# A mixture-of-experts layer: the gate travels with the token's row, and the experts' results are added up in DRAM by the scatters

## The chip, the cores and the metric

The kernel runs on one core of a Trainium2 chip. Its engines are TensorE (PE in the profile, PEld its weight loads), VectorE (DVE), ScalarE (ACT), GpSimd (POOL) and SyncE (SP), which here issues transfers and nothing else. The metric is the device time of one execution in microseconds (us); lower is better.

## What is computed

One transformer layer on `x` of 4 x 1024 tokens with 128 values each, all in float32. First attention with a window of 64 keys is added to `x`. Then a feed-forward part, of which this case changes the end. With `xf` the normalised tokens (N = 4096):

```python
shared = silu(xf @ sg) * (xf @ su) @ sd                  # 128 -> 256 -> 128, every token
top_scores, top_idx = top_k(masked, 4)                   # 4 of 32 experts per token
gates = softmax(top_scores)
pos = cumsum(onehot, 0)[arange(N * K), flat_e] - 1       # place in the expert's queue
keep = pos < capacity                                    # capacity = 640
buf = zeros((E + 1, capacity, d)).at[e_s, p_s].set(xf[tok])[:E]
h = silu(einsum('ecd,edh->ech', buf, wg)) * einsum('ecd,edh->ech', buf, wu)
out_e = einsum('ech,ehd->ecd', h, wd)
contrib = out_e[flat_e, minimum(pos, capacity - 1)] * (flat_g * keep)[:, None]
routed = zeros_like(xf).at[tok].add(contrib)
return x + shared + routed
```

So each of the 32 experts works on up to 640 rows, and a token's output is the sum of at most four experts' rows, each times its gate.

## The kernel before, in words

Each engine has its own program, written by hand in order, and semaphores are the only ties between them. `wait_ge(s, n)` holds an engine's queue until the semaphore has reached n. There are three stages.

**Attention and dispatch.** `attention_steps` walks over 32 tiles of 128 tokens in a software pipeline. For each tile VectorE also picks the four experts and computes the slot numbers `sidx`, and the gates into an SBUF table `gates` (L1155). The normalised row, followed by one more number that tells where its result is to go (the "pair", 4 x token + k, L435), is written by GpSimd with four indirect transfers per tile (`expert_slots<-xfe`, L447) into a table in DRAM with 640 slots of 129 values for each expert. A slot beyond the capacity is out of bounds and is dropped. Beforehand SP fills the table (L320, 32 transfers) and zeroes a second one, `pair_results` with 16384 rows of 128 (L323, 32 transfers).

**Experts.** `lagged_steps` walks over the 32 experts, with three of them in work: for the next one (`en`) TensorE transposes its rows (L875) and VectorE and ScalarE split rows and weights into high and low parts; for the present one (`e`) TensorE does gate and up (L864) in two halves, with SiLU on ScalarE (L607) and the product on VectorE (L1259); for the one before (`ed`) TensorE does the down projection (L890) into PSUM banks 6 and 7 and signals `down_done`. Then ScalarE copies the result out in two pieces (L623 of 512 columns and L625 of 128, both counting `y_evac`), between its two pairs of SiLUs. ScalarE waits there for `down_done`, and for `y_sent`, which tells that the results of two experts ago have left the same buffer. GpSimd waits for both copies and for `yidx`, the destinations as whole numbers (L1265), and issues five indirect transfers of 128 rows (L463), one for each fifth of the 640 slots. Unused slots have a destination out of bounds and are skipped. SP reloads slots, gate/up weights and down weights (L315, L308, L309, L312) in two buffers; ahead of L312 it waits for `down_done` alone.

**Last stage.** The shared expert is computed in eight steps of 512 tokens (`shared_step`). Two are done before the experts, six behind them. SP waits for all scatters and then loads `pair_results` back, four rows for each token, 16 transfers of 512 KB through four buffers (L364). VectorE's `combine` multiplies the first two rows of a token by their gates and adds them to `x_all` (L1246, four for each pair of tiles); GpSimd does the same for the other two (L474, L479, L483), and VectorE adds its sum (L1251). ScalarE's queue stores each pair of tiles (L636, 16 transfers).

## Time and profile before

| | before |
|---|---|
| three runs, us | 888.08, 897.61, 899.48 |
| median | 897.61 |
| span of the profiled execution | 904.6 |
| busy in it: TensorE, VectorE, ScalarE, GpSimd | 724.0, 534.0, 360.9, 415.1 |
| moved between DRAM and the core | 68.37 MB in 52338 packets |
| written to and read from DRAM | 39.99 and 34.89 MB |

The profiled execution is one more run of the same program. Its own time is the span, from the first to the last instruction, and what lies around it, which isn't listed; the runs are below the span by 5 to 17 us. A view that lists groups gives the busy time and the mean of one instruction, and behind the second bar the idle time of the engine just before them and what ended it. "remote" there is a release that the view can't put down to an instruction of this core. The end of a TensorE record is a model, since matmuls overlap.

### The profile page before, as it was taken

Reading aid. Unit: us, or ns where it says so; the run is one execution under the profiler, and the core shown is the slowest. Engines: PE = TensorE matmul, PEld = TensorE weight load, DVE = VectorE, ACT = ScalarE, POOL = GpSimd, SP = SyncE. Lnnn points to the kernel's source line nnn. Section 1 sums busy time; section 2 is a strip of 40 time slices with the busy share of each in tenths; the row PEclk is TensorE's granted clock in tenths of the full one; section 3 lists DMA queues with packets and bytes.
Section 4 is the critical chain, followed back from the end, with each engine's and each line's share of the span. In section 5 each row is a group of like instructions: output and inputs, shape, how many; then the busy total and the mean of one; then the engine's idle time right before and its main releaser. Section 6 shows DMA issues by size and latency. Waiting matters only on the chain.

```text
span 904.6 us, 24570 instructions
## 1 busy us (share of the span) xinstructions
PE 724.0 (80%) x7521; PEld 563.5 (62%) x7521; DVE 534.0 (59%) x2192; ACT 360.9 (40%) x853; POOL 415.1 (46%) x548
## 2 busy tenths in 40 slices
PE   3798888988978788898888858888888888877960
PEld 1565656665646565575665637777777777777540
DVE  3476756556577676656666656545454454543598
ACT  4465544454455445444454423332323232322200
POOL 4125343353343434334344350555555555556555
PEclk9698776676798878767788859999999999998985
DMA  8991000000000000000000002423233333421355
GB/s 268 358 390 35 14 20 15 12 23 12 12 22 10 20 9 15 10 7 14 6 7 6 6 8 84 125 76 105 76 114 107 114 115 103 126 75 32 122 182 167
DMA packets 52338, 68.37 MB, mean 76 GB/s; under 512 B 9505, under 2 KB 31807, under 8 KB 52304
## 3 DMA queue, kind: packets, MB, share of 16 engines
q1 hardware_dynamic: 38240, 53.56, 18.4%
q0 software_dynamic: 9216, 11.97, 4.4%
q10 hardware_dynamic: 4848, 2.40, 0.9%
q8 instruction: 19, 0.31, 0.1%
q14 instruction: 15, 0.12, 0.0%
HBM read 34.89 MB, written 39.99 MB: 83 GB/s over the span
## 4 chain that ended last, share of the span: by engine, by line
PE 52%; another core or an unknown queue 19%; issue 10%; DVE 10%; ACT 6%; POOL 1%; ACTq 1%; DVEq 1%; POOLq 0%
PE bank L693 9%; PE bank L864 7%; PE bank L680 6%; PE bank L674 5%; PE bank L663 5%; PE bank L657 3%; PE bank L701 3%; DVE x_all L1246 3%; DVE mx L1044 2%; PE bank L733 2%; ACT hact L607 2%; PE bank L817 2%; PE bank L756 1%; PE bank L747 1%
## 5 line engine op out<-in xcount | busy, mean ns | idle before, releaser
L463 POOL DMA_INDIRECT pair_results<-yout,yidx x160 | 157.2, 982 | 143.4 <-ACT yout L625 104.0
L447 POOL DMA_INDIRECT expert_slots<-xfe,sidx x128 | 127.0, 992 | 141.5 <-DVE sidx L1148 108.3
L864 PE MATMUL bank<-xgT_parts,wgu_parts 128*128 128x320 f32 x768 | 147.2, 344 | 46.4 <-ACT hact L607 46.4
L864 PEld LDWEIGHTS bank<-xgT_parts,wgu_parts 128*128 128x128 f32 x768 | 125.9, 208 | 57.3 <-ACT hact L607 50.3
L519 ACT ACTIVATE pt<-bank 128x512 f32<-128x512 f32 x128 | 76.2, 596 | 182.2 <-PE bank L680 164.9
L1259 DVE TENSOR_TENSOR hact<-hact,bank 128x320 f32<-128x320 f32 x128 | 57.1, 481 | 140.2 <-ACT hact L607 133.1
L1044 DVE TENSOR_REDUCE mx<-bank 128x4 f32<-128x512 f32 x128 | 87.3, 683 | 32.5 <-PE bank L663 19.7
L421 POOL TENSOR_TENSOR pout<-pin,mhalf 128x3 f32<-128x3 f32 (+2 forms) x36 | 29.9, 830 | 127.4 <-DVE pin L970 127.4
L890 PE MATMUL bank<-wdn,hact 128*128 128x128 f32 x640 | 82.7, 288 | 2.3 <-issue 2.3
L890 PEld LDWEIGHTS bank<-wdn,hact 128*128 128x128 f32 x640 | 82.5, 207 | 2.5 <-issue 2.5
L623 ACT COPY yout<-bank 128x512 f32<-128x512 f32 x32 | 18.7, 585 | 162.2 <-remote 151.0
L657 PE MATMUL bank<-maskq_b,ident_b 128*128 128x512 bf16 x128 | 54.2, 424 | 33.3 <-DVE mx L1044 28.8
L693 PE MATMUL bank<-pt,v_mix 128*32 128x64 f32 x1024 | 78.2, 298 | 0.0
L693 PE MATMUL bank<-pt,v_cur 128*32 128x64 f32 x1024 | 77.0, 293 | 0.0
L607 ACT ACTIVATE hact<-bank 128x320 f32<-128x320 f32 x128 | 53.5, 447 | 38.9 <-PE bank L864 36.7
L680 PE MATMUL bank<-qT,kT 64*128 64x64 bf16 x1024 | 66.7, 218 | 0.1
L674 PE MATMUL bank<-comb_mv,comb_st 112*128 112x128 bf16 x512 | 66.0, 270 | 0.1
L680 PEld LDWEIGHTS bank<-qT,kT 64*128 64x128 bf16 x1024 | 48.4, 111 | 20.2 <-issue 14.4
L663 PEld LDWEIGHTS bank<-kT,qT 64*64 64x64 bf16 x1024 | 37.3, 117 | 37.5 <-issue 37.5
L663 PE MATMUL bank<-kT,qT 64*64 64x128 bf16 x1024 | 60.3, 242 | 0.0
L693 PEld LDWEIGHTS bank<-pt,v_cur 128*32 128x32 f32 x1024 | 54.7, 164 | 0.0
L693 PEld LDWEIGHTS bank<-pt,v_mix 128*32 128x32 f32 x1024 | 49.3, 143 | 3.8
(148 smaller groups left out, 1335.1 us busy)
## 6 DMA issues: line engine op xcount, KB each, us to landing
expert_slots<-fill SPq DMA_DIRECT2D x32, 322.5 KB, 6.5
xg<-expert_slots SPq DMA_DIRECT2D x32, 322.5 KB
pair_results<-rload SPq DMA_DIRECT2D x32, 256.0 KB
rload<-pair_results SPq DMA_DIRECT2D x16, 512.0 KB, 4.0
wgu<-in_L_ffn_wg_dram SPq DMA_DIRECT2D x32, 128.0 KB
wgu<-in_L_ffn_wu_dram SPq DMA_DIRECT2D x32, 128.0 KB
wdn<-in_L_ffn_wd_dram SPq DMA_DIRECT2D x32, 128.0 KB
pair_results<-yout,yidx POOLq DMA_INDIRECT x160
```

What stands on the lines that cost most here:

```text
L447: g.indirect_dma_start(out=slots_d, out_offset=bass.IndirectOffsetOnAxis(ap=sidx[:, tr.b, k:k + 1], axis=0), in_=xfe[:, tr.b, k, :], in_of ...
L463: g.indirect_dma_start(out=pairs_d, out_offset=bass.IndirectOffsetOnAxis(ap=yidx[:, c, j:j + 1], axis=0), in_=yout[:, c, j, :], in_offset= ...
L519: a.activation(pt[:, ts.b, u], bank[2 + u % 2][:, :], ACT.Exp, scale=QK_SCALE)\
L607: a.activation(hact[:, e.b, h, ch * CH:(ch + 1) * CH], bank[2 + h][:, 0:CH], ACT.Silu)\
L657: mm(bk[:, :].rearrange("p (c j) -> p c j", c=4), ident_b[:, :], maskq_b[:, :].unsqueeze(1).broadcast_to([P, 4, P]), start=True, stop=Fals ...
L663: last = mm(bk[hb * WIN:(hb + 1) * WIN, c * P:(c + 1) * P], qT[rows, tp.b, g4 + c, hb * WIN:(hb + 1) * WIN], kT[rows, tp.b, g4 + c, hb * W ...
L674: mm(bk[:, c * P:(c + 1) * P], comb_st[0:WIN + 3 * H, NS * (g4 + c) + s, :], comb_mv[0:WIN + 3 * H, ts.b, :], start=(c == 0), stop=False, ...
L680: last = mm(bk[:, at:at + WIN], kT[rows, ts.b, g4 + c, hb * WIN:hb * WIN + P], qT[rows, ts.b, g4 + c, hb * WIN:(hb + 1) * WIN], start=Fals ...
L693: last = mm(bank[7][32 * (h % 4):32 * (h % 4 + 1), to:to + WIN], vals, pt[:, ts.b, u, at:at + WIN], start=True, stop=True)
L864: last = mm(bank[2 + 2 * w + h][:, 0:CH], wgu_parts[:, e.b, wp, w, h * P:(h + 1) * P], xgT_parts[:, e.b, xp, ch * CH:(ch + 1) * CH], start ...
L890: last = mm(bank[6 + j // 4][:, j % 4 * D:(j % 4 + 1) * D], hact[:, ed.b, h, j * P:(j + 1) * P], wdn[:, ed.b, h, :], start=(h == 0), stop= ...
L1044: v.tensor_reduce(m[:, g4:g4 + 4, s], bank[u % 2][:, :].rearrange("p (c j) -> p c j", c=4), AX.X, ALU.max).then_inc(S.p1_reduced, 1)
```

## The change

The gate of a pair no longer stays in a table. VectorE writes it into the row that is dispatched (column 129 of now 130), and in the place of the pair's number stands the token's (L435's copy now takes `token`). Empty slots are filled with the number of a spare row behind the tokens and a gate of 0. The expert's ScalarE scales each row by its gate when it copies the result out, in five pieces with the gate as the per-partition scale. The five indirect transfers of an expert then add their rows to one of two tables of token sums in DRAM, the even experts to one and the odd ones to the other, and all 640 rows go each time. GpSimd waits for each piece by itself. The last stage loads two sums for each token in place of four rows, in four chunks of eight tiles, and VectorE adds them. Here is the diff, cut to its core:

```diff
-        "pair": ((np.arange(N // P)[None, :, None] * P + p[:, None, None]) * TOPK + np.arange(TOPK)).reshape(P, -1),
+        "token": p[:, None] * (N // P) + np.arange(N // P)[None, :],
+        "spare": N + np.arange(cap // P)[None, :] * P + p[:, None],
...
-    ROW = D + 1
+    ROW = D + 2
...
+    NACC, NCH = 2, 4
+    TCH = NT // NCH
+    ZEROS = NACC * (NCH + 1)
...
-    pairs_d = nc.dram_tensor("pair_results", [N * TOPK, D], F32, kind="Internal").ap()
+    sums_d = [nc.dram_tensor(f"token_sums{a}", [N + cap, D], F32, kind="Internal").ap() for a in range(NACC)]
+    sums_v = [d[0:N, :].rearrange("(p q t) d -> p q (t d)", p=P, q=NCH) for d in sums_d]
...
-            with sp.Fori(0, NT) as t:
-                sp.dma_start(pairs_v[t], rload[:, 0].rearrange("p k d -> p (k d)")).then_inc(S.zeroed, 16)
+            for a in range(NACC):
+                for q in range(NCH):
+                    sp.dma_start(sums_v[a][:, q, :], sums[:, 0, 0].rearrange("p t d -> p (t d)")).then_inc(S.zeroed, 16)
+                sp.dma_start(sums_d[a][N:N + cap, :].rearrange("(j p) d -> p j d", p=P), sums[:, 0, 0, 0:ST, :])\
+                  .then_inc(S.zeroed, 16)
...
-            for c in range(NR // 2):
-                load_results(c, c)
-            with sp.Fori(0, NT // NR - 1) as i:
-                for c in range(NR // 2):
-                    sp.wait_ge(S.comb_step, CSTEPS * ((NR // 2) * i + (c + 1)))
-                    load_results((NR // 2) * i + (NR // 2 + c), c)
+            for q in range(NCH):
+                for a in range(NACC):
+                    sp.dma_start(sums[:, q, a].rearrange("p t d -> p (t d)"), sums_v[a][:, q, :])\
+                      .then_inc(r_arrived[q], 16)
...
+                    pool.wait_ge(S.gate_done, 2 * tr.n + 2)
...
-                    pool.wait_ge(S.y_evac, 2 * e + 2)
-                    hold(pool)
                     for j in range(ST):
+                        pool.wait_ge(S.y_evac, ST * e + (j + 1))
+                        hold(pool)
                         g.indirect_dma_start(
-                            out=pairs_d, out_offset=bass.IndirectOffsetOnAxis(ap=yidx[:, c, j:j + 1], axis=0),
-                            in_=yout[:, c, j, :], in_offset=None, bounds_check=N * TOPK - 1,
-                            oob_is_err=False).then_inc(y_sent[c], 16)
+                            out=sums_d[c], out_offset=bass.IndirectOffsetOnAxis(ap=yidx[:, c, j:j + 1], axis=0),
+                            in_=yout[:, c, j, :], in_offset=None, bounds_check=N + cap - 1,
+                            oob_is_err=True, compute_op=ALU.add).then_inc(y_sent[c], 16)
...
-                    a.copy(yout[:, ed.b, 0:4], bank[6][:, :].rearrange("p (j d) -> p j d", d=D))\
-                     .then_inc(S.y_evac, 1)
-                    a.copy(yout[:, ed.b, 4:ST], bank[7][:, 0:D].rearrange("p (j d) -> p j d", d=D))\
-                     .then_inc(S.y_evac, 1)
+                    act.wait_ge(S.ypair_ready, ed.n + 1)
+                    hold(act)
+                    for j in range(ST):
+                        a.activation(yout[:, ed.b, j], bank[6 + j // 4][:, j % 4 * D:(j % 4 + 1) * D], ACT.Copy,
+                                     scale=ypair[:, ed.b, j, 1:2]).then_inc(S.y_evac, 1)
...
+            for q in range(NCH):
+                act.wait_ge(S.comb_step, 2 * q + 2)
+                act.dma_start(out_v[:, TCH * q:TCH * (q + 1), :], x_all[:, TCH * q:TCH * (q + 1), :])\
+                   .then_inc(S.stored, 16)
...
-                    v.scalar_tensor_tensor(gates[:, bass.ds(tr.n, 1), :].rearrange("p o k -> p (o k)"), ex4[:, tr.b],
-                                           exr[:, :], keep[:, :], ALU.mult, ALU.mult).then_inc(S.gate_done, 1)
+                    v.tensor_scalar(xfe[:, tr.b, :, D + 1], ex4[:, tr.b], exr[:, :], None, ALU.mult)\
+                     .then_inc(S.gate_done, 1)
...
-                    wait(dve, S.yidx_ready, en.n - 1)
-                    v.tensor_copy(ypair[:, en.b], xg[:, en.b, :, D]).then_inc(S.ypair_ready, 1)
...
+                if en is not None:
+                    wait(dve, S.yidx_ready, en.n - 1)
+                    wait(dve, S.y_evac, ST * (en.n - 1))
+                    v.tensor_copy(ypair[:, en.b], xg[:, en.b, :, D:ROW]).then_inc(S.ypair_ready, 1)
...
+            def combine(q):
+                dve.wait_ge(r_arrived[q], 16 * NACC)
+                dve.wait_ge(S.sh_added, 2 * q + 2)
+                xs = x_all[:, TCH * q:TCH * (q + 1), :]
+                for a in range(NACC):
+                    if a:
+                        dve.wait_ge(S.comb_step, NACC * q + a)
+                    v.tensor_tensor(xs, xs, sums[:, q, a], ALU.add).then_inc(S.comb_step, 1)
...
             def shared_and_combine(m, md):
                 shared_step(m, md)
-                if md is not None and md.n > SHARED_EARLY and md.n < N // 512 - 1:
-                    q = 2 * (md.n - SHARED_EARLY - 1)
-                    dve.wait_ge(S.sh_added, md.n)
-                    combine(q, q % (NR // 2), q // (NR // 2))
-                    combine(q + 1, (q + 1) % (NR // 2), (q + 1) // (NR // 2))
+                if md is not None and md.n % 2:
+                    combine(md.n // 2)
+            combine(0)
             shared_steps(shared_and_combine, SHARED_EARLY, N // 512)
```

Line numbers differ between the kernels: the copies L623 and L625 become L605, the scatter L463 becomes L460, `combine` is L1224, the shared step's product L1225 becomes L1206, its addition L1230 becomes L1211, and the SiLU L607 becomes L586.

On ScalarE this stands in the expert loop between the two pairs of SiLUs (first pair's second SiLU, copies, second pair's first). Before:

```order
L607 ACTIVATE hact<-bank 128x320 [waits gu_done]
L244 REGISTER_ALU [waits down_done]
L623 COPY yout<-bank 128x512 [waits y_sent0]
L625 COPY yout<-bank 128x128
L606 REGISTER_ALU
L607 ACTIVATE hact<-bank 128x320 [waits gu_done]
```

And now:

```order
L586 ACTIVATE hact<-bank 128x320 [waits gu_done]
L243 REGISTER_ALU [waits down_done]
L605 ACTIVATE yout<-bank,ypair 128x128 [waits y_sent0,ypair_ready]
L605 ACTIVATE yout<-bank,ypair 128x128 x4
L585 REGISTER_ALU
L586 ACTIVATE hact<-bank 128x320 [waits gu_done]
```

The two copies of different size have become five of the same, and the first of them waits for `ypair_ready` as well.

On GpSimd the expert loop reads so before, from the end of the dispatch on (the two experts of a turn):

```order
L456 UNCONDITIONAL_BRANCH [waits zeroed]
L456 ISA
L460 ISA [waits yidx_ready]
L463 DMA pair_results<-yout,yidx 16384x128 [waits y_evac]
L463 DMA pair_results<-yout,yidx 16384x128 x4
L459 REGISTER_ALU
L460 ISA [waits yidx_ready]
L463 DMA pair_results<-yout,yidx 16384x128 [waits y_evac]
```

And now, for the first of the two experts:

```order
L452 UNCONDITIONAL_BRANCH [waits zeroed]
L452 ISA
L458 ISA [waits yidx_ready]
L460 DMA token_sums<-yout,yidx 4736x128 [waits y_evac]
L458 REGISTER_ALU
L460 DMA token_sums<-yout,yidx 4736x128 [waits y_evac]
L458 REGISTER_ALU
L460 DMA token_sums<-yout,yidx 4736x128 [waits y_evac]
L458 REGISTER_ALU
L460 DMA token_sums<-yout,yidx 4736x128 [waits y_evac]
```

One wait for the copies ahead of five transfers has become a wait ahead of each, with a register step between two transfers.

On VectorE this is the way from the last expert (first row) into the last stage. Before:

```order
L1259 TENSOR_TENSOR hact<-hact,bank 128x320 [waits gu_done,h_act] x4
L1265 CAST yidx<-ypair 128x5 [waits y_sent1,ypair_ready]
L1225 TENSOR_TENSOR sact<-sact,bank 128x512 [waits sh_gu,sh_act] x4
L1230 TENSOR_TENSOR x_all<-x_all,bank 128x512 [waits sh_down]
L1225 TENSOR_TENSOR sact<-sact,bank 128x512 [waits sh_gu,sh_act] x2
L1230 TENSOR_TENSOR x_all<-x_all,bank 128x512 [waits sh_down]
L1246 SCALAR_TENSOR_TENSOR x_all<-rload,gates,x_all 128x128 [waits r_arrived0,sh_added]
L1246 SCALAR_TENSOR_TENSOR x_all<-rload,gates,x_all 128x128
L1246 SCALAR_TENSOR_TENSOR x_all<-rload,gates,x_all 128x128 [waits comb_step] x2
L1251 TENSOR_TENSOR x_all<-x_all,rload 128x256 [waits late_sum,comb_step]
```

And now:

```order
L1232 TENSOR_TENSOR hact<-hact,bank 128x320 [waits gu_done,h_act] x4
L1238 CAST yidx<-ypair 128x5 [waits y_sent1,ypair_ready]
L1224 TENSOR_TENSOR x_all<-x_all,sums 128x1024 [waits sh_added,r_arrived0]
L1224 TENSOR_TENSOR x_all<-x_all,sums 128x1024 [waits comb_step]
L1206 TENSOR_TENSOR sact<-sact,bank 128x512 [waits sh_gu,sh_act] x4
L1211 TENSOR_TENSOR x_all<-x_all,bank 128x512 [waits sh_down]
L1206 TENSOR_TENSOR sact<-sact,bank 128x512 [waits sh_gu,sh_act] x2
L1211 TENSOR_TENSOR x_all<-x_all,bank 128x512 [waits sh_down]
L1224 TENSOR_TENSOR x_all<-x_all,sums 128x1024 [waits sh_added,r_arrived1]
L1224 TENSOR_TENSOR x_all<-x_all,sums 128x1024 [waits comb_step]
```

The first two additions of loaded sums have moved ahead of all products and additions of the late shared steps; the four small multiply-adds and one addition for a pair of tiles have become two additions of 1024 columns for eight tiles.

## Rows read from the trace of the kernel before

**Rows 1.** Sums by stretch, experts and last stage: busy us of each engine, clock, DMA, GB/s

```profile
540.00:830.00 290.00, 241.05 (x1591) 224.70 (x1590) 140.10 (x355) 89.97 (x223) 151.37 (x154) 0.92 0.32 97
830.00:905.00 75.00, 40.09 (x171) 26.43 (x170) 55.01 (x101) 9.13 (x18) 41.83 (x58) 0.77 0.46 143
```

**Rows 2.** Waits, 480 to 830, and SP's: who for whom, us, times, longest

```profile
ACT yout L623 <- remote: 151.0, 29, 5.7
...
SPq L312 <- remote: 192.5, 29, 8.5
```

**Rows 3.** Timeline of one round: start, us, engine, line, names, count, idle before

```profile
653.39 0.58 ACT L623 COPY yout<-bank 128x512 f32<-128x512 f32 x1 [4.68 <-remote]
653.45 0.38 SPq L312 DMA_DIRECT2D wdn<-in_L_ffn_wd_dram  x1
653.87 0.27 ACT L625 COPY yout<-bank 128x128 f32<-128x128 f32 x1
...
654.16 0.34 SPq L315 DMA_DIRECT2D xg<-expert_slots  x1
...
654.61 0.88 DVE L1259 TENSOR_TENSOR hact<-hact,bank 128x320 f32<-128x320 f32 x2 [4.45 <-ACT hact L607]
...
654.98 0.97 POOL L463 DMA_INDIRECT pair_results<-yout,yidx  x1 [2.70 <-ACT yout L625]
...
656.57 2.39 PE L890 MATMUL bank<-wdn,hact 128*128 128x128 f32 x20
...
660.11 0.97 POOL L463 DMA_INDIRECT pair_results<-yout,yidx  x1 [0.30 <-issue]
...
660.56 0.71 PE L875 MATMUL bank<-cst,xg 128*128 128x128 f32 x5
...
662.24 0.58 ACT L623 COPY yout<-bank 128x512 f32<-128x512 f32 x1 [5.47 <-remote]
```

**Rows 4.** Timeline, the first expert behind the loop

```profile
829.03 0.97 POOL L463 DMA_INDIRECT pair_results<-yout,yidx  x1 [0.30 <-issue]
829.68 0.59 ACT L623 COPY yout<-bank 128x512 f32<-128x512 f32 x1 [2.89 <-PE bank L890]
...
831.13 0.44 ACT L607 ACTIVATE hact<-bank 128x320 f32<-128x320 f32 x1 [0.70 <-PE bank L864]
```

**Rows 5.** Timeline, last scatter, loads, and the start of two late shared steps

```profile
845.16 0.97 POOL L463 DMA_INDIRECT pair_results<-yout,yidx  x1 [0.30 <-issue]
...
845.88 1.02 PE L837 MATMUL bank<-xfT_all,sgw 128*128 128x512 f32 x2
...
847.37 45.29 SPq L364 DMA_DIRECT2D rload<-pair_results  x16
...
851.10 1.02 PE L837 MATMUL bank<-xfT_all,sgw 128*128 128x512 f32 x2
```

**Rows 6.** Groups by form: the scatters (480 to 830), VectorE in the last stage

```profile
L463 POOL DMA_INDIRECT pair_results<-yout,yidx x150 | 147.5, 983 | 137.0 <-ACT yout L625 100.0 <-issue 37.0
...
L1246 DVE SCALAR_TENSOR_TENSOR x_all<-rload,gates,x_all 128x128 f32<-128x128 f32 x32 | 18.9, 649 | 0.0
...
L1230 DVE TENSOR_TENSOR x_all<-x_all,bank 128x512 f32<-128x512 f32 x6 | 4.1, 681 | 3.1 <-PE bank L847 3.1
```

**Rows 7.** Timeline, the last instruction

```profile
901.76 0.42 DVE L1251 TENSOR_TENSOR x_all<-x_all,rload 128x256 f32 x1
```

**Rows 8.** Sums by stretch in the last stage (clock, DMA share, GB/s at the end)

```profile
850.00:856.00 6.00, 6.00 (x34) 4.09 (x33) 4.94 (x9) 1.19 (x2) 4.11 (x7) 1.00 0.76 288
...
860.00:864.00 4.00, 3.91 (x6) 1.77 (x7) 3.97 (x11) 0.60 (x1) 2.62 (x6) 0.62 0.36 131
```

**Rows 9.** DMA queues and issues: median us to landing at the end of a row

```profile
q0 software_dynamic: 9216, 11.97, 4.4%
...
rload<-pair_results SPq DMA_DIRECT2D x16, 512.0 KB, 4.0
...
wout<-in_L_attn_Wout_dram ACTq DMA_DIRECT2D x1, 64.0 KB, 3.5
```

More of the change, by code:

```diff
@@ L136, in block_kernel @@
         numbers = field("numbers")
-        pair = field("pair").rearrange("p (t k) -> p t k", k=TOPK)
+        token = field("token")
+        spare = field("spare")
         wqkv = sb("wqkv", [P, 3 * D])
```

79 lines of the change are left out of this document (16 added, 63 removed).

## The prediction, made before the changed kernel was run

> **What bounds the kernel now.** I read the spans first, then the sums by stretch, the list of waits, the timeline of the expert loop, the groups by form and the timeline of the last stage. The profiled span is 904.6 us; the three runs took 888.08 to 899.48 us with median 897.61, which is 7.0 below the span. I make my sum against the span and take 7.0 off. Attention and dispatch fill the time up to 540 us, and nothing in the change sits on their path. The experts fill 540 to 830, the last stage 830 to 905, where TensorE is busy for 40 of 75 us and VectorE for 55 [rows 1].
>
> In the expert loop one expert takes 8.9 us: from the first copy of ScalarE (L623) at 653.39 to the next at 662.24 [rows 3]. TensorE's records end long before that: the down projections run from 656.57 to 658.96, the transposes of the next expert end at 661.3, yet ScalarE sits until 662.24 [rows 3]. The list of waits gives ScalarE 29 such waits, 151.0 us, with a releaser called "remote", and the load of the down weights on SP's queue 29 as well [rows 2]. What both wait for is `down_done`, the semaphore of the last down matmul: SP's L312 starts within 0.06 us of L623 and has no other wait there [rows 3]. So it is TensorE's signal that comes late. When does it come? The five scatters (L463) start 1.59 us after L623 and then every 1.28 us. The fifth ends at 661.08, and 1.16 us later ScalarE goes on [rows 3]. At 829.68, the first expert behind the loop, the copy is released by its down matmul while a batch is still going; but the next SiLU (L607) is then held until 831.13, 1.13 us after that batch's last scatter ends at 830.00 [rows 4]. And the last scatter of all ends at 846.13 and has landed when SP issues its loads at 847.37, 1.24 us later [rows 5]. I read from this that a batch of scatters in flight holds TensorE's signals back until it has landed. The round is a ring then: copy, 1.59 us to the first scatter, four times 1.28 and 0.97 us of scatters, 1.16 us of landing, copy. That makes 8.84 of 8.85 us.
>
> The last stage begins with that landing at 847.3. It has 16 loads of 512 KB (4.0 us to landing [rows 9]) and five additions on VectorE for each, the last one starting at 901.76 [rows 7]. Its bound is VectorE: the multiply-adds alone (L1246), 64 of about 0.6 us, take over 34 us [rows 6]. From 847.3 to 904.6 are 57.3 us.
>
> **Last stage: what changes.** Eight loads of 512 KB in place of 16, and eight additions of 128x1024. One of 128x256 with nothing beside it takes 0.42 us [rows 7], one of 128x512 0.68 us [rows 6]; the slope of 1.02 ns makes 1.2 us for 1024. So VectorE has some 10 us of additions in place of over 40, and GpSimd's multiplications go. But the order of the program moves work too. `combine(0)` now stands ahead of the six late shared steps on VectorE, and they queue behind its wait for both y_sent and two loads. Before, these steps filled that wait; the third of the late ones starts at 851.10 [rows 5]. Now TensorE will do the gate and up matmuls of one late step, begin the next and stop, since the product of the first (L1206) isn't made. I count from the landing L. The first pair of loads: 4.0, and 1.8 for the second 512 KB at the 288 GB/s of the stretch 850 to 856 [rows 8, 9], with the issue 5.9. Two additions: 8.4. Products and hand-over 0.8: 9.2. A late step takes 5.2 us, the distance from 845.88 to 851.10, and one of the four pairs of its gate and up matmuls under 1 (1.02 with its overlap) [rows 5]. So the rest of the step that stopped takes 4.4, and 2 more because TensorE has stood still, as after its pause before 860, when the granted clock was 0.62 over 4 us, a mean between 2.4 and 1.2 GHz [rows 8]. Four more steps: 20.9. The last down projections, about a third of a step: 1.9, so L + 38.4. Then 0.7 and 2.4 us of additions with hand-overs: 41.6. A store of 512 KB at the load's 4.0: L + 45.7. The last stage gets 57.3 - 45.7 = **11.6 us** shorter. It isn't halved, because TensorE becomes its bound and starts late.
>
> **Expert loop: what changes in a round.** (a) GpSimd waits for one slice instead of two copies. L625 starts 0.48 us behind L623 and is itself 128 wide [rows 3]; a first slice in its place lets the first scatter go 0.48 earlier. ScalarE first has one more wait and one more instruction that holds; I allow 0.13. Gain **0.35**. (b) Between the scatters stand a wait and a no-operation. The slices come faster (0.27 us each [rows 3]) than the scatters, so the wait is met. The gap of 0.30 may grow by 0 to 0.1; I take 0.05 four times, **0.2**. (c) Five slices of 0.27 cost ScalarE some 1.0 us with their overlap, 0.4 more than the two copies, and the SiLUs behind start so much later. In this ring TensorE has that to spare before its signals are let go: nothing; if the ring were gone, 0.4 a round. (d) The copy of `ypair` moves to the end of VectorE's step, and SP's load of the next slots waits for it. The load went at 654.16; behind the two products (L1259, to 655.49) it will go some 1.6 later. Its first use are the transposes at 660.56 [rows 3], so 4.8 us are left for a transfer of about 4. Nothing, but less than 1 us of cover is left. The wait for `y_evac` at that place is met, since the products ahead need SiLUs that follow the copies. (e) The scatter becomes an addition in DRAM. The trace has none. It has two prices: time on GpSimd and time to landing. On GpSimd the plain one takes 0.98 us [rows 6]. Low end 0 more, high end twice the work, +0.98 a scatter. I take 0, as the plain row is the nearest. To landing the low end is 0. At the high end stands a whole small transfer more, since the old sum must come out of DRAM before the new one goes in: a 64 KB load has 3.5 us from issue to landing [rows 9]. I take one more trip as long as the present landing, **1.2**, because the issue's part of the 3.5 isn't paid twice. Only the fifth scatter's counts, as the others land under their successors. All 640 rows of a batch now go, where about 57% did: 11.97 MB [rows 9] are 11,640 rows moved twice (516 and 512 bytes), and there are 20,480 slots. That lies within the range of (e).
>
> Sum of a round: -0.35 + 0.2 + 1.2 = **+1.05 us**, for 31 rounds **+32.5 us**.
>
> The Trainium skill bears on (e). Its page "DMA: Bandwidth & Descriptors" (Anatomy of one DMA) says that most of a transfer's fixed time is the wait until the target memory confirms the write. The 1.24 us behind the last scatter agree in kind; by the page's fixed 2.0 us an estimate of the extra trip would be 2.0 instead of 1.2, and the total 25 us more.
>
> **The rest.** Zeroing shrinks from 8.4 MB to 4.8, and only weight loads stand behind it that are needed after 540 us. The fill waits for one small copy on GpSimd more, behind memsets, at the very start. The gate of a tile is made on VectorE just ahead of its slot numbers, for which GpSimd waits anyway. All nothing. Total: 904.6 + 32.5 - 11.6 = 925.5, less 7.0: **919 us**.
>
> **Rivals.**
> 1. *Plain price* (faster or about the same). The addition lands as quickly as a copy. A round then gains 0.15, 31 of them 4.7; with 11.6 that is 16: 881. Should the late shared steps not wait for the loads, up to 12 more, 869. For it: the scatter's time now hardly varies. Against: the old sum must be read somewhere.
> 2. *The ring opens* (faster). Additions in flight don't hold TensorE's signals. A round is then TensorE's work, 241 us by 32 or 7.5 us [rows 1], plus (c): 7.9. Saved are 1.0 x 31 and 11.6: 855. Nothing in the trace speaks for it but that it doesn't tell why the signals wait.
> 3. *A slow landing* (slower). 2 to 3.5 us more a round in place of 1.2: 944 to 990. For it: the 3.5 us of a small load.
> 4. *A slow scatter* (slower). GpSimd takes the middle of my two ends, 1.47 us a scatter: 2.4 us a round, 76 us on the forecast, 995. From +0.2 a scatter (31 us, 950) it outweighs by far what the last stage can give. For it: the five scatters are 6.1 of the ring's 8.85 us and nothing hides them. Against: the plain row. The Trainium skill's same page gives one read and one write descriptor for an operation (SWDGE vs HWDGE vs iDMA), and has the adding unit combine two streams (SDMA does more than copy): by this three descriptors in place of two. No row here shows it.
>
> **How the numbers follow.** The forecast, with a landing 0.6 to 1.8 us longer (900 to 938): 0.34. Rival 1: 0.24. Rival 2: 0.08. Rival 3: 0.14. Rival 4 of any size: 0.20. The range for eight in ten runs from 868, which takes in rival 1, to 990, which leaves out rival 2 and the upper part of rival 4. The likeliest case's own range is 900 to 938. About 2% either way (880 to 916) can't be told from no change. Faster: rival 2, most of rival 1, whose 881 is on the line, and no more: 0.26. Same: the rest of rival 1 and the lower part of the forecast: 0.26. Slower: 0.48.
>
> **What would show it.** ScalarE's wait before L605 ends 1.2 us (rival 1) or 2.4 us (forecast) after the fifth scatter. The scatter's mean is 0.98 us (forecast) or 1.2 and more (rival 4). From one expert to the next are 9.9 us (forecast), 8.7 (rival 1) or below 8 (rival 2). In the last stage TensorE stands for some 12 us behind one late step, `combine(0)` goes first on VectorE, and the end comes 46 us after the last landing. I would be wrong most simply if TensorE's late signals have another cause than the scatters, or if the price of an addition falls on the transfer queues all along and not at the end.

## The result, and the profile after

The changed kernel took 921.0 us (median of 4 runs, 918.68 to 924.18) where the kernel before took 894.68 (4 runs): a ratio of 1.032, 95% interval 1.024 to 1.040, so it is slower. The forecast said 919. That the number agrees is luck: the mechanism behind it was another one than the forecast's, and this document is mostly about that. The two traces are compared below stretch by stretch. The execution that the trace of before shows is a long one, with a span 10 us above that kernel's median, while the span of the changed kernel is 2.8 below its own. So the traces differ by 13.6 us and the medians by 26.3, and no trace shows where the other 12.7 us lie.

First the page of the changed kernel: span, busy times, DMA queues, the chain by engine, and the groups of the scatters and of ScalarE's slices.

```profile
span 918.2 us, 24411 instructions
...
PE 729.6 (79%) x7521; PEld 569.6 (62%) x7521; DVE 499.3 (54%) x2120; ACT 387.3 (42%) x949; POOL 478.2 (52%) x501
...
q0 software_dynamic: 27136, 16.54, 14.2%
...
PE 54%; issue 16%; POOL 7%; DMA 7%; DVE 7%; ACT 5%; another core or an unknown queue 2%; POOLq 1%; DVEq 1%; ACTq 0%; SPq 0%
...
L460 POOL DMA_INDIRECT token_sums<-yout,yidx x160 | 251.7, 1573 | 68.7 <-issue 41.1
...
L605 ACT ACTIVATE yout<-bank,ypair 128x128 f32<-128x128 f32 x160 | 44.7, 371 | 91.7 <-DMA token_sums<-yout,yidx 56.7
```

A scatter takes GpSimd 1573 ns, where it took 983 [rows 6]. The queue q0 has 27,136 packets in place of 9216 [rows 9]. ScalarE's slices take 371 ns each.

Now the waits and the sums by stretch: the expert loop, the first loads of the last stage, and the rest of it. The columns are those of [rows 2] and [rows 1].

```profile
DVE yidx L1238 <- DMA token_sums<-yout,yidx: 131.8, 30, 6.3
...
ACT yout L605 <- DMA token_sums<-yout,yidx: 56.7, 17, 6.9
ACT yout L605 <- PE bank L871: 32.6, 14, 2.4
POOL token_sums L460 <- issue: 41.1, 135, 0.3
```

```profile
570.00:870.00 300.00, 226.95 (x1498) 215.45 (x1496) 126.55 (x328) 112.09 (x310) 251.55 (x160) 0.89 0.61 103
871.80:879.30 7.50, 0.00 (x0) 0.00 (x0) 0.00 (x0) 0.00 (x0) 0.00 (x0) 0.50 0.80 273
879.30:918.20 38.90, 28.81 (x134) 18.66 (x134) 21.62 (x26) 5.37 (x9) 0.00 (x0) 0.89 0.33 110
```

The "remote" waits of ScalarE in front of its copies, 151.0 us [rows 2], are gone. In their place ScalarE and VectorE wait for scatters of two experts ago, and GpSimd waits for nobody: its 160 scatters take 251.55 of 300 us, and what is left is the 0.30 us between two of them. One expert is five scatters with their gaps, 5 x (1.57 + 0.30) = 9.4 us, and from 569.96 to 871.84 are 301.9 us, 32 x 9.43. So the loop is bound by the issue of scatters on GpSimd, and no longer by a ring.

The timeline shows the same at one copy, and then the end (PE is the matmul record, the bracket is the idle time before it).

```profile
589.37 2.39 PE L871 MATMUL bank<-wdn,hact 128*128 128x128 f32 x20
590.42 1.54 POOL L460 DMA_INDIRECT token_sums<-yout,yidx  x1 [0.30 <-issue]
...
591.88 1.40 ACT L605 ACTIVATE yout<-bank,ypair 128x128 f32<-128x128 f32 x5 [2.31 <-PE bank L871]
592.26 1.54 POOL L460 DMA_INDIRECT token_sums<-yout,yidx  x1 [0.30 <-issue]
...
868.58 1.54 POOL L460 DMA_INDIRECT token_sums<-yout,yidx  x1 [0.30 <-issue]
...
871.84 4.91 SPq L364 DMA_DIRECT2D sums<-token_sums  x8
879.33 2.48 DVE L1224 TENSOR_TENSOR x_all<-x_all,sums 128x1024 f32<-128x1024 f32 x2 [25.75 <-DMA sums<-token_sums]
...
882.46 2.08 PE L821 MATMUL bank<-xfT_all,suw 128*128 128x512 f32 x2 [26.01 <-DVE sact L1206]
...
888.44 1.02 PE L818 MATMUL bank<-xfT_all,sgw 128*128 128x512 f32 x2
...
893.66 1.02 PE L818 MATMUL bank<-xfT_all,sgw 128*128 128x512 f32 x2
...
912.10 2.48 DVE L1224 TENSOR_TENSOR x_all<-x_all,sums 128x1024 f32<-128x1024 f32 x2
```

The down matmuls end at 591.76 and ScalarE starts at 591.88 while scatters follow each other without a break: here TensorE's signal is not held by scatters in flight. The last scatter ends at 870.12, and SP issues its loads at 871.84, 1.7 us later, where it was 1.24 [rows 5]. From there to the end of the span are 46.4 us, where they were 57.2.

### The profile page after: what moved, and what is told of

Its sections match the earlier page's. It is cut to its first block, busy times and chain, and to the rows that moved or that the text cites. A ratio compares the mean times of both kernels' runs of the same rounds, so it can differ in the third digit from the quotient of the medians.

```text
span 918.2 us, 24411 instructions
## 1 busy us (share of the span) xinstructions
PE 729.6 (79%) x7521; PEld 569.6 (62%) x7521; DVE 499.3 (54%) x2120; ACT 387.3 (42%) x949; POOL 478.2 (52%) x501
## 3 DMA queue, kind: packets, MB, share of 16 engines
q0 software_dynamic: 27136, 16.54, 14.2%
## 4 chain that ended last, share of the span: by engine, by line
PE 54%; issue 16%; POOL 7%; DMA 7%; DVE 7%; ACT 5%; another core or an unknown queue 2%; POOLq 1%; DVEq 1%; ACTq 0%; SPq 0%
PE bank L674 10%; DMA token_sums<-yout,yidx 6%; PE bank L644 6%; PE bank L661 6%; POOL token_sums L460 6%; PE bank L655 6%; PE bank L845 5%; PE bank L638 4%; PE bank L682 3%; PE bank L714 2%; DVE mx L1025 2%; PE bank L871 2%; PE bank L828 2%; PE bank L821 2%
## 5 line engine op out<-in xcount | busy, mean ns | idle before, releaser
L460 POOL DMA_INDIRECT token_sums<-yout,yidx x160 | 251.7, 1573 | 68.7 <-issue 41.1
L845 PE MATMUL bank<-xgT_parts,wgu_parts 128*128 128x320 f32 x768 | 154.3, 350 | 56.6 <-DVE hact L1232 53.5
L845 PEld LDWEIGHTS bank<-xgT_parts,wgu_parts 128*128 128x128 f32 x768 | 130.7, 215 | 64.3 <-DVE hact L1232 60.1
L586 ACT ACTIVATE hact<-bank 128x320 f32<-128x320 f32 x128 | 56.2, 444 | 90.3 <-PE bank L845 89.7
L605 ACT ACTIVATE yout<-bank,ypair 128x128 f32<-128x128 f32 x160 | 44.7, 371 | 91.7 <-DMA token_sums<-yout,yidx 56.7
L674 PE MATMUL bank<-pt,v_mix 128*32 128x64 f32 x1024 | 80.3, 304 | 0.0
L674 PE MATMUL bank<-pt,v_cur 128*32 128x64 f32 x1024 | 79.4, 300 | 0.0
L1238 DVE CAST yidx<-ypair 128x5 uint32<-128x5 f32 x32 | 7.1, 222 | 131.8 <-DMA token_sums<-yout,yidx 131.8
L871 PE MATMUL bank<-wdn,hact 128*128 128x128 f32 x640 | 76.6, 275 | 0.7 <-issue 0.7
L871 PEld LDWEIGHTS bank<-wdn,hact 128*128 128x128 f32 x640 | 75.0, 192 | 0.9 <-issue 0.9
```

The lines of the kernel that those rows point to most:

```text
L460: g.indirect_dma_start(out=sums_d[c], out_offset=bass.IndirectOffsetOnAxis(ap=yidx[:, c, j:j + 1], axis=0), in_=yout[:, c, j, :], in_offse ...
L674: last = mm(bank[7][32 * (h % 4):32 * (h % 4 + 1), to:to + WIN], vals, pt[:, ts.b, u, at:at + WIN], start=True, stop=True)
L845: last = mm(bank[2 + 2 * w + h][:, 0:CH], wgu_parts[:, e.b, wp, w, h * P:(h + 1) * P], xgT_parts[:, e.b, xp, ch * CH:(ch + 1) * CH], start ...
L871: last = mm(bank[6 + j // 4][:, j % 4 * D:(j % 4 + 1) * D], hact[:, ed.b, h, j * P:(j + 1) * P], wdn[:, ed.b, h, :], start=(h == 0), stop= ...
```

## The experiments

**The kernels ran under other conditions than in the first comparison.** In all three later comparisons the kernel before took 725 to 726 us, not 895. So the kernel before and the changed one were run again, unchanged, and each experiment is held against these.

Two lengths will tell nearly everything: the *loop*, from the first scatter of the results to SP's first load of the last stage, and the *last stage*, from there to the end of the span. They are differences of times in each timeline.

| kernel | us, median | ratio to before (95%) | first scatter | loop | last stage |
|---|---|---|---|---|---|
| before, first comparison | 894.7 | | 566.0 | 281.4 | 57.2 |
| changed, first comparison | 921.0 | 1.032 (1.024 to 1.040) | 570.0 | 301.9 | 46.4 |
| before_again | 725.3 | | 456.7 | 209.6 | 57.2 |
| after_again | 804.8 | 1.109 (1.103 to 1.116) | 453.8 | 302.0 | 45.5 |
| after_copy | 712.4 | 0.981 (0.975 to 0.986) | 456.3 | 212.5 | 45.8 |
| after_half | 804.9 | | 457.5 | 300.0 | 45.6 |
| after_four | 743.1 | 1.022 (1.015 to 1.029) | 456.4 | 240.0 | 45.7 |
| after_late | 792.2 | 1.092 (1.086 to 1.098) | 455.0 | 303.6 | 32.3 |
| before_pieces | 722.6 | 0.996 (0.993 to 0.999) | 457.0 | 207.7 | 56.4 |
| before_four | 715.5 | 0.987 (0.982 to 0.993) | 456.4 | 199.9 | 57.2 |
| before_two | 714.1 | 0.985 (0.979 to 0.991) | 451.3 | 196.8 | 60.7 |
| gated_pairs | 705.8 | 0.975 (0.968 to 0.981) | 453.9 | 213.2 | 36.2 |
| gated_again | 704.9 | 0.968 (0.963 to 0.974) | 462.0 | 211.8 | 36.3 |

The last three columns are read from one trace of each kernel. The loop of after_again and that of after_late are the same code and differ by 1.6 us, so a difference of 2 or 3 us between two loops is hardly more than scatter.

**1. Both kernels again.** No edit.

> The kernel before, unchanged, for its trace where it takes 725 us and not 895. Theory A (the ring belongs to the first comparison alone: there a wait of TensorE's signals until the scatters had landed stood in the trace; here the kernel is 170 us faster): the waits for a releaser that the trace cannot name, 19% of the chain of before, are gone, the expert loop takes 6.5 to 6.7 us a round in place of 8.85, TensorE is its bound, and the last stage still takes 57 us. Theory B (all of it is a higher clock of TensorE from the start): the unnamed releaser keeps its share, and the round is 8 us or more.

> The changed kernel, unchanged, under the same conditions as the other experiments. Theory A (GpSimd's 5 x 1.88 = 9.4 us bounds its round in either condition; the kernel before is bound by TensorE at 6.6 us a round here): the loop takes 300 us as with the combining step placed late, the last stage 46 us, so about 804 us, 1.11 of before. Theory B (placing the combining step late has cost time, and not saved any): 780 us or less.

Both theories A held. First the kernel before in the first comparison: the chain by engine, and a stretch of attention in the sums by stretch.

```profile
PE 52%; another core or an unknown queue 19%; issue 10%; DVE 10%; ACT 6%; POOL 1%; ACTq 1%; DVEq 1%; POOLq 0%
```

```profile
100.00:400.00 300.00, 255.69 (x3323) 180.16 (x3322) 194.81 (x1011) 148.17 (x353) 125.18 (x187) 0.78 0.05 15
```

The same kernel in before_again: chain and scatters of its page, the sums of the same stretch and of the expert loop, and the timeline of one copy.

```profile
PE 47%; issue 20%; DVE 12%; POOL 10%; ACT 5%; DMA 4%; DVEq 1%; POOLq 1%; ACTq 0%; SPq 0%
...
L463 POOL DMA_INDIRECT pair_results<-yout,yidx x160 | 157.4, 984 | 72.2 <-issue 47.4
```

```profile
100.00:400.00 300.00, 273.74 (x4480) 194.19 (x4474) 273.59 (x1343) 194.01 (x470) 169.63 (x251) 0.99 0.06 17
457.00:665.00 208.00, 203.60 (x1520) 195.67 (x1518) 132.90 (x331) 93.68 (x216) 157.08 (x161) 1.00 0.43 127
```

```profile
458.94 2.39 PE L890 MATMUL bank<-wdn,hact 128*128 128x128 f32 x20
...
460.50 1.26 POOL L463 DMA_INDIRECT pair_results<-yout,yidx  x1 [0.30 <-issue]
461.37 0.59 ACT L623 COPY yout<-bank 128x512 f32<-128x512 f32 x1 [2.23 <-PE bank L890]
```

In the first comparison, two of the waits of attention with the unnamed releaser, the first from before and the second from the changed kernel:

```profile
ACT pt L519 <- remote: 17.2, 5, 4.1
```

```profile
ACT oT L526 <- remote: 7.9, 4, 2.6
```

In before_again the unnamed releaser is gone from the chain. A scatter lasts as long as before (984 against 983 ns), but the same 300 us of attention hold 4480 matmuls in place of 3323, with a granted clock of 0.99 in place of 0.78. The down matmuls end at 461.33, a scatter is being issued, and the copy starts at 461.37. So plain scatters in flight don't hold TensorE's signal here, and TensorE is busy for 203.6 of 208 us of the loop. Of the 181 us that the kernel before is faster here, 109 lie ahead of the first scatter and 72 in the loop; the last stage is the same 57.2. The changed kernel gains ahead of the first scatter only (116 us); its loop stays at 302.0 against 301.9. Up to the first scatter the kernel before had such unnamed waits in the first comparison too, on ScalarE and VectorE, 45.5 us in all, and the changed kernel 22.5; before_again and after_again have none. GpSimd's issue is a bound of its own, whatever TensorE does.

**2. The addition alone.**

```diff
                             in_=yout[:, c, j, :], in_offset=None, bounds_check=N + cap - 1,
-                            oob_is_err=True, compute_op=ALU.add).then_inc(y_sent[c], 16)
+                            oob_is_err=True).then_inc(y_sent[c], 16)
```

> The changed kernel with plain scatters: the addition is left out of them, so that of several rows for one token only the last to land stays, and the sums are not the reference's. Nothing else differs: as many scatters, rows, waits and loads. Theory A (the addition itself costs GpSimd time: 1573 ns a scatter against 983 ns before, and five scatters with their gaps, 5 x 1.88 = 9.4 us, are the round): a scatter falls back to about 0.98 us, GpSimd's part of a round to 5 x 1.28 = 6.4 us, and the round to the ring of the forecast without its landing term, 8.5 to 8.9 us, 893 to 905 us in all; if the ring stays open, the round is 7.7 us or so and the time about 869. Theory B (the scatter is longer because all 640 rows are now sent and none is skipped): it stays at 1.5 to 1.6 us and the time at 915 to 925. Theory C, my forecast's landing term (the addition costs 1.2 us where the fifth scatter lands, and nothing on GpSimd): scatter unchanged at 1.57, landing 1.2 us earlier.

Queue and scatters on the page of after_copy, and the sums of its loop:

```profile
q0 software_dynamic: 9216, 16.54, 6.8%
...
L460 POOL DMA_INDIRECT token_sums<-yout,yidx x160 | 162.7, 1017 | 70.8 <-issue 36.3
```

```profile
456.00:668.00 212.00, 199.28 (x1500) 192.80 (x1499) 124.44 (x328) 107.98 (x311) 162.68 (x160) 1.00 0.48 147
```

Theory A: with the same rows and bytes a plain scatter takes 1.02 us, and the loop 212.5 us. Without the addition the loop is 89.5 us shorter, and the whole change would be 1.9% faster than before (1.4 to 2.5%). The round of 6.6 us (212.5 / 32) is shorter than either that I had named, since those were for 895 us. Sending all 640 rows, the longer slices, the waits between scatters and the moved copy together cost at most some 3 us of loop (212.5 against 209.6). Behind the last scatter, which ends at 667.42, the loads go at 668.76, 1.34 us later; the adding kernels have 1.55 to 1.91. The other plain ones have 1.21 to 1.25, but before_pieces, whose scatters are plain as well, has 1.86 (662.79 to 664.65). So it is not shown that the addition costs landing time; at most it is some 0.2 to 0.7 us, once a batch. What it costs on GpSimd is shown: 0.56 us for each scatter.

**3. What the price goes by.** Adding scatters of half a row; the tables are seen as rows of 256 B and the row numbers are doubled.

```diff
-                            out=sums_d[c], out_offset=bass.IndirectOffsetOnAxis(ap=yidx[:, c, j:j + 1], axis=0),
-                            in_=yout[:, c, j, :], in_offset=None, bounds_check=N + cap - 1,
+                            out=sums_d[c].rearrange("n (h d) -> (n h) d", h=2), out_offset=bass.IndirectOffsetOnAxis(ap=yidx[:, c, j:j + 1], axis=0),
+                            in_=yout[:, c, j, 0:D // 2], in_offset=None, bounds_check=2 * (N + cap) - 1,
```

> The changed kernel with adding scatters of half a row, 256 B in place of 512 B: the second half of every result is left out of the sums. As many scatters, row numbers and packets. Theory A (GpSimd's 1541 ns for an adding scatter, against 972 ns for a plain one, is a price for each row, since the adding one sends one packet for each row, and the plain one one for four): it stays at 1.54 us and the loop at 300 us. Theory B (the price is for the bytes that are read, added and written back): a scatter falls by about half of the 0.57 us, to 1.25 us, the round to 7.8 us and the loop to 250 us.

Queue and group of the scatters:

```profile
q0 software_dynamic: 27136, 11.30, 13.4%
```

```profile
L460 POOL DMA_INDIRECT token_sums<-yout,yidx x160 | 250.0, 1563 | 72.3 <-issue 40.8 <-ACT yout L605 30.8 <-DVE yidx L1238 0.6
```

Theory A: 1563 ns for half the bytes, and 804.9 us (one run). The price isn't for bytes. What does change with the addition is the number of packets. Queue q0 of after_four and of before_four (both are experiment 4, with 32 scatters fewer):

```profile
q0 software_dynamic: 22528, 14.44, 14.4%
```

```profile
q0 software_dynamic: 8192, 10.78, 4.9%
```

The 32 adding scatters were 4608 packets, so one of 128 rows is 144; the 32 plain ones were 1024, so one is 32. That GpSimd's time goes by packets is argued from this, not shown: a kernel with another number of rows in a scatter wasn't tried.

The Trainium skill's page "Perfetto Trace Analysis" (DMA Instruction, SWDGE) says that such an instruction's end in the profile is the moment when the last descriptor has been generated, not when the data has moved. The rows agree: half the bytes leave 1563 ns, and the landing comes 1.5 us and more behind the record's end.

**4. One scatter fewer**, in the changed kernel and in the one before (there also three fewer).

```diff
-                    for j in range(ST):
+                    for j in range(ST - 1):
```

The waits for `y_sent` count four as well (before_two: two).

> The changed kernel with four of the five adding scatters of each expert; the fifth, of an expert's last 128 slots, is left out, with its results. Theory A (GpSimd's row of scatters is the round): it loses 1.88 us x 32 = 60 us against the changed kernel, a round of 7.5 us. Theory B (the round is set by the landing and the two tables' turns: copy, scatters, landing, copy into the same buffer two experts later): it loses the same scatter but a further share of slack stays, 30 to 50 us. With the four scatters of the kernel before the loss was 9 us only, as TensorE is its bound.

> The kernel before with four of the five scatters of each expert; the fifth, of an expert's last 128 slots, is left out, with its results. Theory A (the ring of the forecast: copy, five scatters in a row, landing, TensorE's signal, copy): a round loses one scatter with its gap, 1.28 us, x 31 = 40 us, 853 to 858 us. Theory B (the round is set by TensorE's or VectorE's work, and the scatters lie beside it): 890 to 897 us. In between, another bound stands behind the ring, and the time says where: a round of 8.2 us would give 874.

> The kernel before with two of the five scatters of each expert; the results of an expert's last 384 slots are left out. If the kernel before takes 725 us in this comparison, Theory A (TensorE bounds the expert loop): about what four scatters gave, 0.98 to 0.99 of before, as there is no ring to shorten. If it takes 895 us, the ring of the forecast (copy, scatters, landing, TensorE's signal, copy) loses 3 x 1.28 us a round until TensorE's own 6.3 us bound it, so 2.5 us x 31 = 78 us, 0.91 of before; against it Theory B (TensorE's signals are late for a reason of their own, and not held by the scatters): 0.98 to 1.00 there too.

The changed kernel loses 62.0 us of loop, which is 32 x 1.94: every scatter taken away is gained in full, and Theory A holds. The kernel before loses 9.7 us of loop with one scatter fewer and 12.8 with three (where the last stage gives 3.5 back). My ring would have given 40 with one, so Theory B is the nearer for before_four, though it allowed 5 us at most, and for before_two Theory A holds: there is no ring in these conditions. TensorE is the bound that remains, by the sums of a stretch of before_four:

```profile
457.00:648.00 191.00, 190.31 (x1482) 189.74 (x1481) 130.89 (x326) 89.81 (x209) 128.31 (x123) 1.00 0.44 131
```

In this stretch of before_four TensorE is busy for 190.31 of 191 us. Of the kernel before's 6.55 us a round (209.6 / 32), five scatters with their gaps are 6.4: two bounds stand side by side, and taking one scatter away gains only the 0.3 us a round by which the loop lies above TensorE's own (199.9 / 32 = 6.25 us). That is why a scatter that is 0.56 us longer costs nearly its whole price: 5 x 0.56 x 32 = 90 us, where 89.5 were measured.

**5. The evacuation alone**, in the kernel before.

```diff
-                    pool.wait_ge(S.y_evac, 2 * e + 2)
-                    hold(pool)
                     for j in range(ST):
+                        pool.wait_ge(S.y_evac, ST * e + (j + 1))
+                        hold(pool)
...
-                    a.copy(yout[:, ed.b, 0:4], bank[6][:, :].rearrange("p (j d) -> p j d", d=D))\
-                     .then_inc(S.y_evac, 1)
-                    a.copy(yout[:, ed.b, 4:ST], bank[7][:, 0:D].rearrange("p (j d) -> p j d", d=D))\
-                     .then_inc(S.y_evac, 1)
+                    for j in range(ST):
+                        a.copy(yout[:, ed.b, j], bank[6 + j // 4][:, j % 4 * D:(j % 4 + 1) * D])\
+                         .then_inc(S.y_evac, 1)
```

> The kernel before with the change's evacuation alone: ScalarE copies the five slices one by one, GpSimd waits for each slice ahead of its scatter, scatters are plain and go to the pair rows, and the last stage is that of before. The forecast's terms for this: -0.35 us a round for the first scatter that starts earlier, +0.2 us for waits between scatters, 31 rounds: -4.7 us, so 890 us. Theory A (as the trace of after shows, the ring opened: TensorE's signal for the products no longer waits for the scatters' landing): the round falls from 8.9 to below 8.5 us, and the time to 865 to 885. Theory B (ScalarE's five short copies take longer in all than two long ones and lie in the ring): 895 to 905.

The ratio 0.996 is a small gain at best; the traces have 1.9 us less of loop and 0.8 of last stage, which is within scatter. The expected times were made for 895 us, and as there was no ring this run can't say what the slices do to one. The gap between scatters stays at 0.30 us with a wait in it, so the forecast's +0.2 a round was nothing.

**6. The last stage.** VectorE's first combining step behind the late shared steps 2 and 3, not ahead of them.

```diff
             def shared_and_combine(m, md):
                 shared_step(m, md)
+                if md is not None and md.n == 3:
+                    combine(0)
                 if md is not None and md.n % 2:
                     combine(md.n // 2)
 
-            combine(0)
             shared_steps(shared_and_combine, SHARED_EARLY, N // 512)
```

> The changed kernel with the first combining step of VectorE placed behind the late shared steps 2 and 3 and not ahead of them. Theory A (TensorE stands for 26 us in the last stage since VectorE waits for the first sums, loaded 8 us after the last landing, before it does the product of a late shared step): the late shared steps run while the sums load, TensorE's stand falls under 10 us, and the stage becomes 35 to 38 us instead of 46.4, so 910 to 913 us. Theory B (the late shared steps cost 5.2 us each by TensorE's own work and its clock, and the first of them cannot start earlier, as the stand is GpSimd's and the last landings'): 918 to 922 us.

The timeline behind the last landing:

```profile
758.62 4.35 SPq L364 DMA_DIRECT2D sums<-token_sums  x8
...
764.36 2.48 DVE L1224 TENSOR_TENSOR x_all<-x_all,sums 128x1024 f32<-128x1024 f32 x2 [9.01 <-DMA sums<-token_sums]
...
770.32 2.07 PE L821 MATMUL bank<-xfT_all,suw 128*128 128x512 f32 x2 [9.61 <-DVE sact L1206]
```

Theory A, and more than it had: the stage is below its 35 to 38 us. TensorE stands for 9.6 us in place of the 26 of the changed kernel in the first comparison (24.3 in after_again), the last stage is 32.3 us in place of 45.5, and the time 12.6 us less. `combine(0)` ahead of the shared steps was a cost of the change that had nothing to do with the two sums.

**7. The gate with the row, and plain scatters.** From the changed kernel: the row carries the pair's number again, the scatters copy into one row for each pair, eight loads of 1 MB bring them back in the order in which the new layout has each partition's rows together, and VectorE adds four of them to each token, the first chunks each behind a late shared step from the fourth on and the rest at the end.

```diff
-        "token": p[:, None] * (N // P) + np.arange(N // P)[None, :],
+        "pair": ((p[:, None, None] * (N // P) + np.arange(N // P)[None, :, None]) * TOPK + np.arange(TOPK)).reshape(P, -1),
...
-                            out=sums_d[c], out_offset=bass.IndirectOffsetOnAxis(ap=yidx[:, c, j:j + 1], axis=0),
+                            out=pairs_d, out_offset=bass.IndirectOffsetOnAxis(ap=yidx[:, c, j:j + 1], axis=0),
...
+                if q >= NRB:
+                    sp.wait_ge(S.comb_step, TOPK * (q - NRB + 1))
+                sp.dma_start(sums[:, q % NRB].rearrange("p t k d -> p (t k d)"), pairs_v[:, q, :])\
+                  .then_inc(r_arrived[q % NRB], 16)
...
+                for k in range(TOPK):
+                    if k:
+                        dve.wait_ge(S.comb_step, TOPK * q + k)
+                    v.tensor_tensor(xs, xs, sums[:, q % NRB, :, k], ALU.add).then_inc(S.comb_step, 1)
```

> Half of the change, rearranged: the gate travels with the row, ScalarE scales five slices, GpSimd scatters each as it comes, but by plain copies into one row for each token and expert choice, as before. The last stage loads these 8.4 MB in eight loads of 8 KB for each partition, and VectorE adds four of them to each token with four adds of 512 elements, behind the late shared steps. Theory A (the addition in the scatter is what costs; the rest of the change costs nothing): the loop is that of before, 205 us, and the last stage goes by its loads, 8.4 MB at some 190 GB/s = 44 us and 6 us behind them, 50 us in place of 58: 712 to 717 us. Theory B (the last stage is bound by VectorE's adds and the waits between them): 57 us or more, 720 to 728 us.

> The rearranged kernel a second time (gate with the row, five slices, plain scatters to the pair rows, eight wide loads and plain adds behind the late shared steps). If before takes 725 us, 0.97 to 0.98 of it, as the first time. If it takes 895 us: the loop keeps the ring, 8.7 us a round, or opens it as the five slices do under the changed kernel; with the ring it gains the last stage alone, 20 us, 0.975 to 0.98 of before; with the ring open, up to 60 us more, 0.91.

It took 705.8 us, 0.975 of before, and in the third comparison 704.9, a ratio of 0.968 (0.963 to 0.974). No other version is faster. The second time it lies just below the 0.97 to 0.98 that I had expected. Sums of the last stage, and VectorE's adds, from gated_pairs:

```profile
666.00:703.00 37.00, 20.88 (x107) 13.84 (x105) 29.24 (x45) 4.18 (x7) 0.00 (x0) 0.82 0.83 285
```

```profile
L1219 DVE TENSOR_TENSOR x_all<-x_all,sums 128x512 f32<-128x512 f32 x32 | 21.8, 690 | 3.0 <-DMA sums<-pair_results 2.1
```

The loop is 213.2 us, that of after_copy within 1, and the last stage 36.2 us in place of 57.2. I had expected a loop of 205 and a last stage of 50, with 8.4 MB at 190 GB/s. The stretch moves 285 GB/s, its stores among them, and 32 adds take VectorE 21.8 us where the kernel before has over 34 us of multiply-adds [rows 6]. Against after_late the last stage is 3.9 us longer with twice the bytes to load; `combine(0)` at its early place cost 13.2. Which part of the 21 us comes from wider loads, which from plain adds without gates, and which from their place was not tried.

## Why the prediction was right, and where it was wrong

Against the span the forecast was 925.5 us, and the changed kernel's span was 918.2. The loop took 301.9 where 281.4 + 32.5 = 313.9 were forecast: 12.0 less. The last stage took 46.4 where 45.7 were forecast, and the first scatter came 4.0 later, of which the forecast had nothing; on the later runs it came 2.9 us earlier, so I take this for scatter between runs. That makes -7.3. The forecast then took 7.0 off for the median, while the median lay 2.8 above the span. So 919 and 921 agree because misses had opposite signs: 7 us in the span and 10 between span and median. That is luck, and so is the loop's part of it, as the next points show. By the prediction's own signs it was rival 4 that came: it put "1.2 and more" for the scatter's mean, and 1.57 us was measured.

**(e), GpSimd's part: "I take 0, as the plain row is the nearest".** This is the step that failed. It measured +0.59 us a scatter in the first comparison and +0.56 between after_copy and after_again. Rival 4 named this mechanism, and its end of 1.47 us is near the measured 1.57. Of the two ends, nothing and twice the work, the plain row was the nearest in form and the wrong one; my only reason against rival 4 was the plain row, and the trace of before has no adding scatter.

**(e), the landing: +1.2 us a round.** It measured 1.7 - 1.24 = 0.5 at the last batch, and even this may not be the addition's, as before_pieces has 1.86 with plain scatters. It isn't on the path of the loop, since GpSimd is never idle for more than 0.30 us. Only in the last stage does it count, once. The 2.0 us that the prediction worked out by the Trainium skill's page "DMA: Bandwidth & Descriptors" for the extra trip are farther off still.

**The ring.** The trace of before had it: 8.84 us of 8.85 were accounted for. But it belonged to the conditions of that comparison, and it was gone from the changed kernel even there: a signal came 0.12 us behind its matmul with scatters in flight. So rival 2, to which I gave 0.08 because nothing spoke for it, happened as well. The price of rival 4 alone, 5 x 0.59 = 3.0 us a round on the ring, would have given some 94 us more in the loop. What came was +0.6 us a round where +1.05 was forecast: from the ring's 8.8 (281.4 / 32) to GpSimd's 9.4. Under the later conditions, with no ring to open, the full price stands: 302.0 against 209.6.

What held TensorE's signals in the first comparison stays open. Plain scatters in flight can't be enough, as before_again shows. Whether they do it only under those conditions and adding ones don't, or whether the cause is another that came and went with the scatters' timing, could not be tried: all later runs were made where the kernel before took 725 us. The unnamed waits in attention, where no result is scattered yet, speak for another cause; but the scatters of the dispatch are in flight there. That attention was slow in both kernels of the first comparison (first scatter at 566.0 and 570.0, against 451 to 462 later) says that the conditions, not the change, brought it.

**(a) and (b).** The first scatter starts 1.21 us behind the first slice (568.75 to 569.96), in place of 1.59: 0.38, forecast 0.35. The gaps stayed 0.30: forecast +0.2 a round, measured nothing. Neither is on the path. **(c)** Five slices take 1.40 us together (371 ns each with the scale, forecast some 1.0), where two copies took 0.75; before_pieces without the scale cost nothing, after_copy with it lost 3 us of loop with all its other differences. **(d)** The move of the `ypair` copy cost nothing visible: in the first comparison the transposes wait for no load.

**The last stage** came out right, -10.8 against -11.6 us, and by its own steps nearly: two additions take 2.48 us (forecast 2.4), a late step 5.22 (5.2), TensorE goes on at L + 10.6 (forecast 9.2, since the loads land 7.5 us after L and not 5.9), the last additions end at L + 42.7 (41.6). TensorE stood for 26 us and not 12: it had finished its experts long before GpSimd, so the stand began earlier, and it ends where the forecast said. The cause given, `combine(0)` ahead of the late steps, is shown by after_late: 13.2 us. The forecast saw this order and its cost (up to 12 us, in rival 1); the change without it is 12.6 us faster.

## What to carry to other kernels

Ask of a scatter what it costs the engine that issues it before asking what it costs the queues: here the adding one took 1.57 us of GpSimd for 128 rows whatever the row's length, and with five for each expert that was the bound of the whole loop. A wait with an unnamed releaser may belong to the conditions of one run; a forecast that rests on it should carry a second sum without it, and here that second sum (7.5 us a round of TensorE, as in rival 2, and 6.4 of GpSimd) says that from 0.22 us more a scatter GpSimd is the bound even without the ring. And take a change apart: the gate with the row, wider loads and plain adds behind the late steps were together worth 21 us of last stage, and the addition in the scatter cost 90 of loop.

## What the runs showed of the hardware that I had not expected

- An adding indirect scatter of 128 rows takes GpSimd 1.56 to 1.58 us on average for rows of 512 B and of 256 B alike, a plain one 0.97 to 1.05. It puts 144 packets into its queue in place of 32.
- SP goes on 1.55 to 1.91 us behind the end of the last adding scatter's record, and 1.21 to 1.34 behind a plain one's in seven traces, but 1.86 in before_pieces.
- The same kernel took 895 us in one comparison and 725 in three others, with its scatters of the same length (983 and 984 ns). With the longer time went TensorE's late signals (19% of the chain has a releaser that the trace can't name, and before_again has none) and a lower granted clock, 0.78 against 0.99 in the same 300 us of attention. Which of them, if either, brought the other isn't shown.
- The changed kernel's loop took 301.9 us in the first comparison and 302.0 later. A kernel bound by an engine that the disturbance doesn't touch hides it.
